# Attention with a routed feed-forward on one core: weights fetched at another round, late projections in halves, first value sets spread

## The chip, the cores and the metric

The kernel runs on one core of one Trainium2 chip. The metric is the device time of one execution in microseconds (us); lower is better. Inputs are float32 and lie in the chip's memory (HBM).

## What is computed

A layer with two branches on one sequence of 2048 tokens of width 128, cut to what matters:

```python
xn = layernorm(x)                                   # 2048 x 128
mod = cos(phase) * amplitude                        # per head and dimension
q, k, v = (xn @ W).split into 16 heads of 8, times mod
scores = q @ k.T / sqrt(8) * cos(2 pi (i - j) / S)  # 16 heads, 2048 x 2048
w = softmax(scores);  w = (w + roll(w, 1, axis=-1)) / sqrt(2)
attention = (w @ v) @ Wo
logits = small softmax mix of xn @ wqkv.T over 8 experts, top 2 per token
ffn = sum over the 2 chosen experts of score * (silu(xn @ w1a.T) * (xn @ w1g.T)) @ w2.T   # F = 352
out = x + attention + ffn
```

The factor cos(2 pi (i - j)/S) is split as cos i cos j + sin i sin j, so each head has 16 rows of q and k (8 dimensions, two rotations). These are stored as float16 high and low parts, 49 rows with a shift row.

## The kernel before, in words

Engines: PE is the matrix engine, PEld its weight load, ACT the activation engine, DVE the vector engine, POOL the general engine, SP the engine that issues most DMAs. All run their own instruction list in order and meet through semaphores.

**Set-up.** `turn_x` makes xnT, `rotate(n)` on PE (L1171 to L1184) makes sixteen projections: i = n // 4 names one of q and k for the first and the second eight heads, c = n % 4 is a quarter of 512 tokens; each is two matrix multiplications of 64 columns of weights by 512 tokens into a PSUM bank from `PROJ_BANKS`. DVE's `rotate(n)` (L782 to L787) multiplies the bank by `mod_up` and cos/sin into `rotated[i]`. Projections 0 to 11 are made in the set-up. Projections 12 to 15 (k of the second eight heads) are made late, one in each of the rounds 10 to 13 (`LATE_AT`), on both engines. They read xnT.

**The rounds.** Attention has 16 heads with 64 score tiles of 128 x 512 each, 1024 tiles in all. Five PSUM banks form a ring; a round r (0 to 204) handles five tiles. In a round PE runs `scores(2r)` (three tiles, banks 0 to 2) and `scores(2r+1)` (two tiles, banks 3 and 4); ACT's `weights(g)` makes one exponential over each group (128x1536, then 128x1024) into `probs`, a ring of 15 tiles in SBUF (L697). `scores(g)` waits until the exponential of group g - 2 is done. Then PE runs `weighted_values(u)` (L1353 to L1376): a piece u is half of a set of four tiles, 4 matrix multiplications of 256 columns with the values as weights (the first set of each head is one piece of 512 columns, u = 0 being empty). Float32 multiplications are two instructions each. `rounds()` (L350 to L376) says which pieces belong to a round: those up to `even = (RING * HALVES * r - NC) // NC`, so 1, 3, 2, 3, 2, 3 pieces in rounds 1 to 6 and from there on 2 and 3 in turn. From round 6 on it is 3 where r is even. ACT's `weights(g)` also waits for the pieces that read the probs it overwrites, from tile 15 (round 3) on: group 6 needs pieces 0 and 1, group 7 pieces 2 and 3, group 9 pieces 4 and 5.

**Work put into the rounds.** After the scores and before the pieces of a round PE does: `rank_tokens` in round 7, the late projections, `square_sums(1)` in round `SECOND_AT` (sums for the ordering of heads and the shifts) and `turn_other(1)` two rounds on. After the pieces it does the expert work. DVE's list has in each round: squares, `copy_out` and `normalise` of the head before (the latter at set k == 2), expert evacuations, then the late rotation and, in the rounds of `PARTS_AT`, `rest(i)`, which makes the two float16 parts of `rotated[i]`. `normalise` writes `attn`, which lies over xnT. DVE runs freely ahead of the rounds; only its semaphores hold it.

**Experts.** Tokens are sorted into 39 tiles of 128 by expert. POOL's `scatter_rows` (L609) writes them to `slots_x` in HBM, one call for each set of four tiles from set 11 to 42, released by that set's pieces. At round 35 (`EXPERTS_AT - 2`, L515) SP waits for all scatters, issues `load_rows(0)` and `load_rows(1)` (L452, eight DMAs), then `stage_weights(0..2)` (w1 and w2 of the first three tiles, L479 and L480, 544 KB a tile, into `staged`, which lies over the stored float16 parts), then `carried` (L522), which DVE's `rows_of_results` reads at round 40. At round 37 it loads the operands of the two exact heads. PE's `widen(0, 0)` (L1281) comes at the end of round 38 and `widen(0, 1)` at the end of 39: they wait for `staged_ld`, `xgT_ready` (DVE's transposition of the loaded rows, L962) and `order_ready`. An expert tile takes four rounds, so the experts run beside the attention from round 38 to the last.

Of the kernel before, what the change touches and what calls it, by code (L numbers as in the profile page):

```python
# [33 lines left out]
ALU = mybir.AluOpType  # L34
# [11 lines left out]
CW = 512  # L46
NC = S // CW
# [12 lines left out]
RING = LARGE_GROUP + SMALL_GROUP  # L60
# [3 lines left out]
QUADS = PER_HEAD // NC  # L64
HALVES = 2
# [13 lines left out]
TOP_EXP_AT = 7  # L79
RANK_AT = 7  # L80
GATES_AT = 8
SECOND_AT = 22
EXPERTS_AT = 37
SCATTER_AT = 11
ROUNDS_A_TILE = 4
LATE_AT = 10
PARTS_AT = (15, 17)
SQUARES_AT = (19, 20)
HALF_HEADS = H // 2
EARLY = HALF_HEADS - EXACT  # L90
EXACT_AT = 156
# [7 lines left out]
PI_DOWN = 3.1415925  # L99
LOWEST = -3.0e38  # L100
EPS = 1e-5
PROJ_BANKS = (2, 3, 0, 1, 2, 3, 0, 1, 2, 3, 0, 1, 7, 5, 7, 5)
SUM_BANKS = (4, 6, 5, 0)
SPREAD = 4.3
ROOT_GUESS = float(0x5F3759DF)
# [11 lines left out]
def build(nc, x, Wq, Wk, Wv, Wo, phase, amp, wqkv, w1, w2, ident_in, desc_in, cs_in, sel_in, tri_in, below_in, count_in, heads_in, earlier_in, of_head_in, places_in, out):  # L117
# [11 lines left out]
    with ExitStack() as ctx:  # L129
# [224 lines left out]
        def rounds():  # L354

            done, j, taken = 0, 0, [0, 0]
            for r in range(ROUNDS + 1):
                w = done // HALVES
                jobs, p = [], w // QUADS
                wanted = jobs_before(p + 1) - j if w % QUADS >= JOB_QUAD else 0  # L360
                half = (RING * r + 1) % 2
                for _ in range(min(wanted, 2 if wanted > (QUADS - w % QUADS) * NC // RING else 1)):
                    if taken[half] == JOBS // 2:
                        half = 1 - half
                    jobs.append((p, j, *job_in(half, taken[half])))
                    taken[half] += 1
                    j += 1
                ready = min(RING * r, SCORE_TILES) // NC * HALVES
                even = (RING * HALVES * r - NC) // NC
                pieces = range(done, max(ready if r == ROUNDS else min(ready, even), done))  # L370
                done = pieces.stop
                yield r, jobs, pieces
# [27 lines left out]
        def _(sp):  # L400
# [81 lines left out]
            def store_shifts(g):  # L482
                sp.wait_ge(shift_ready, g + 1)
                sp.dma_start(shift_rows[HALF_HEADS * g:HALF_HEADS * g + HALF_HEADS, :].rearrange("h (t p) -> (h t) p", p=P),
                             shift[:, g, :]).then_inc(shift_wr, 16)
# [19 lines left out]
            for r, _, _ in rounds():  # L505
                m, step = expert_step(r)
                for p in range(2, PLAIN):
                    issued = groups_for(PER_HEAD * (p - 1))
                    if r == -(-issued // 2):
                        sp.wait_ge(score_ready, issued)  # L510
                        load_head(p)
                if r - 1 in PARTS_AT:
                    for part in range(2):
                        store_part(2 + PARTS_AT.index(r - 1), part)
                if r == SECOND_AT + 3:  # L515
                    store_shifts(1)
                if r == EXPERTS_AT - 2:
                    load_rows(0)
                    load_rows(1)
                    for first in range(STAGES - 1):  # L520
                        stage_weights(first)
                    sp.dma_start(carried[:], slots_x[0:TILES * P, DM:WITH_PLACE].rearrange("(n p) k -> p n k", p=P)).then_inc(carried_ld, 16)  # L522
                if r == EXPERTS_AT:
                    sp.wait_ge(rows_ready, 2)
                    sp.wait_ge(order_ready, 2)
                    for i in range(EXACT):
                        h = sp.value_load(head_order[0:1, PLAIN + i:PLAIN + i + 1], min_val=0, max_val=H - 1)
                        for half in range(2):
                            load_operands(sp, h, qe[:, i, :], ka[:, 2 + i, :], half, exact_ld)
                if step == 1 and m + STAGES - 1 < TILES:  # L530
                    stage_weights(m + STAGES - 1)
                if step == 1 and m % 2 == 1 and m // 2 + 2 < ROW_PAIRS:
                    load_rows(m // 2 + 2)
                if r == EXACT_AT:
                    load_exact_shifts()
# [193 lines left out]
        def _(dve):  # L729
# [52 lines left out]
            def rotate(n):  # L782

                i, c = n // NC, n % NC
                dve.wait_ge(proj_ps, n + 1)
                nc.vector.scalar_tensor_tensor(rotated[i][:, CW * c:CW * c + CW], ps[:, PROJ_BANKS[n], :], mod_up[:, i // 2:i // 2 + 1],  # L786
                                               cs[:, CW * c:CW * c + CW], ALU.mult, ALU.mult).then_inc(rot_ready, 1)  # L787

            def square_late(i):

# [265 lines left out]
            for r, jobs, pieces in rounds():  # L1056
# [14 lines left out]
                for w in quads_in(pieces):  # L1071
                    p, k = w // QUADS, w % QUADS
                    if p >= 1 and k == 0:
                        copy_out(p - 1)
                    if p == 1 and k == 2:
                        dve.wait_ge(x_kept, 16)
                    if p >= 1 and k == 2:
                        normalise(p - 1)
                    if jobs_before(p) < JOBS and jobs_before(p + 1) == JOBS and k == QUADS - 2:
                        make_exact_shift(p)  # L1080
                    if p == H - 1 and k == ADD_AT:
                        add_results()
# [8 lines left out]
                    take_g(m)  # L1091
                if r == RANK_AT:
                    assign_slots()
                if LATE_AT <= r < LATE_AT + 4:
                    dve.wait_ge(rot_ready, 12 + r - LATE_AT)
                    rotate(12 + r - LATE_AT)
                if r in PARTS_AT:
                    dve.wait_ge(rot_ready, 16)
                    rest(2 + PARTS_AT.index(r))
                if r == GATES_AT:  # L1100
                    place_tokens()
# [56 lines left out]
        def _(pe):  # L1158
# [12 lines left out]
            def rotate(n):  # L1171

                i, c = n // NC, n % NC
                g, which = i // 2, i % 2
                if n < 4:
                    pe.wait_ge(xt_ready, max(c + 1, n + 1))
                elif n < 12:
                    pe.wait_ge(rot_ready, n - 3)
                else:
                    pe.wait_ge(rot_ready, max(n - 1, 12))  # L1180
                    pe.wait_ge(slot_ready, 1)
                for half in range(2):
                    ins = nc.tensor.matmul(ps[64 * half:64 * half + 64, PROJ_BANKS[n], :], wmat[:, which, 64 * g:64 * g + 64],  # L1183
                                           xnT[:, CW * c:CW * c + CW], start=True, stop=True, tile_position=(0, 64 * half))  # L1184
                ins.then_inc(proj_ps, 1)

            def values(t):
# [164 lines left out]
            def weighted_values(u):  # L1352
# [4 lines left out]
                cols = slice(HW * half, HW * half + HW)  # L1357
                if half == 0:
                    pe.wait_ge(exp_done, groups_for(tiles[-1] + 1))
                if u == QUADS * HALVES:  # L1360
                    pe.wait_ge(rot_ready, 16)
                if k == 0 and half == 0:
                    pe.wait_ge(vh_ready, p + 1)
                    after(pe, o_copied, p - 1)
# [37 lines left out]
            for r, jobs, pieces in rounds():  # L1402
# [6 lines left out]
                            max_job(*job)  # L1409
                if r == RANK_AT:  # L1410
                    rank_tokens()
                if LATE_AT <= r < LATE_AT + 4:
                    rotate(12 + r - LATE_AT)
                if r == SECOND_AT:
                    pe.wait_ge(slot_ready, 1)
                    square_sums(1)
# [92 lines left out]
```

## Time and profile before

| | us |
|---|---|
| runs before | 593.88, 595.48, 599.56 (median 595.48) |
| the profiled execution | 593.97 |
| its span (first to last instruction) | 592.2 |
| outside the span | 1.77 |
| PE busy | 543.2 (92%) |
| ACT busy | 520.6 (88%) |
| DVE busy | 223.6 (38%) |
| granted clock of PE over the span | 0.983 |

The profile is of one execution. Times in a row are from the start of the span. A row of the timeline merges neighbouring instructions of one line; the bracket is how long the engine sat idle before, and who released it. The granted clock is a share of 2.4 GHz, 0.50 being 1.2 GHz.

### The profile page before, as it was taken

To read this page: it belongs to the slowest core of one execution; us is meant where nothing else is said; L and a number is where in the kernel's file an instruction comes from. 1 tells how busy PE (TensorE), PEld (TensorE's weight loads), DVE (VectorE), ACT (ScalarE), POOL (GpSimd) and SP (SyncE) were. 2 spreads that over 40 slices of the span, in tenths; PEclk is the share of its full clock that TensorE was granted. 3 is DMA by queue.
4 is the path that set the end of the run, shared out by engine and by line. 5 is a ranking of instruction groups with operands and counts; after the bars stand their busy time and mean duration, and the time that the engine had idled before them with its cause. 6 is when DMAs were issued, how large, how long until landed. Compare 5 with 4: busy or idle time off the path is not lost.

```text
span 592.2 us, 19062 instructions
## 1 busy us (share of the span) xinstructions
PE 543.2 (92%) x7948; PEld 255.3 (43%) x7948; DVE 223.6 (38%) x517; ACT 520.6 (88%) x480; POOL 97.3 (16%) x102
## 2 busy tenths in 40 slices
PE   2867998887999999999999999999999999999884
PEld 1342333332444444444445445444544545454333
DVE  7976346500413434344343434334343212221134
ACT  2648989997899999999999999999999999999991
POOL 5210068543001010010101010010101001010000
PEclk9987999999899999999999999999999999999999
DMA  7852035214644232241423233232323313200402
GB/s 220 175 170 94 1 104 145 87 33 126 144 132 128 62 103 78 78 112 48 131 53 96 85 94 96 85 95 66 98 71 95 95 44 94 54 11 7 147 2 74
DMA packets 60890, 53.76 MB, mean 91 GB/s; under 512 B 33244, under 2 KB 50294, under 8 KB 60546
## 3 DMA queue, kind: packets, MB, share of 16 engines
q1 hardware_dynamic: 58082, 47.48, 30.2%
q0 software_dynamic: 2272, 4.72, 2.2%
q8 instruction: 65, 1.06, 0.8%
q10 hardware_dynamic: 448, 0.30, 0.2%
q14 instruction: 23, 0.19, 0.1%
HBM read 38.68 MB, written 13.78 MB: 89 GB/s over the span
## 4 chain that ended last, share of the span: by engine, by line
PE 67%; ACT 13%; issue 11%; DVE 4%; DMA 3%; SPq 1%; POOL 0%; ACTq 0%; DVEq 0%
PE ps L1374 33%; PE ps L1348 21%; ACT big L697 11%; PE ps L1281 7%; PE ps L1291 4%; DMA qk_parts<-store 1%; DVE attnT L761 1%; PE ps L1183 1%; DMA acc<-in_L_attn_x 1%; PE ps L1318 1%; ACT store L654 1%; SPq L452 1%; DMA store<-in_L_ffn_w 1%; DVE big L786 0%; DMA slots_x<-attnT,slot 0%
## 5 line engine op out<-in xcount | busy, mean ns | idle before, releaser
L697 ACT ACTIVATE big<-ps 128x1536 f32<-128x1536 f32 (+1 forms) x410 | 481.4, 1236 | 28.8 <-PE ps L1348 24.7
L1374 PE MATMUL ps<-big,vh 128*32 128x256 f32 (+1 forms) x3968 | 265.7, 394 | 0.0
L1348 PE MATMUL ps<-qa,ka 49*128 49x512 f16 x896 | 166.0, 388 | 19.7 <-ACT big L697 12.9
L1374 PEld LDWEIGHTS ps<-big,vh 128*32 128x32 f32 x3968 | 108.6, 110 | 113.9 <-issue 65.5
L1348 PEld LDWEIGHTS ps<-qa,ka 49*128 49x128 f16 x896 | 37.5, 94 | 139.2 <-ACT big L697 107.5
L593 POOL DMA_INDIRECT results<-y,row_of x39 | 37.9, 971 | 270.8 <-DVE y L984 269.4
L1281 PE MATMUL ps<-xgT,store 128*32 128x128 f32 x1716 | 66.5, 276 | 2.8 <-DMA store<-in_L_ffn_w 2.8
L1281 PEld LDWEIGHTS ps<-xgT,store 128*32 128x32 f32 x1716 | 55.0, 112 | 18.4 <-issue 6.0
L969 DVE SCALAR_TENSOR_TENSOR cs<-cs,ps 128x384 f32<-128x384 f32 x39 | 21.6, 554 | 91.9 <-ACT cs L689 91.9
L1047 DVE TENSOR_REDUCE m<-ps 128x1 f32<-128x512 f32 x64 | 44.1, 689 | 31.2 <-PE ps L1385 31.2
L984 DVE TENSOR_SCALAR y<-ps,weight_of 128x128 f32<-128x128 f32 x39 | 13.7, 351 | 98.2 <-PE ps L1291 98.2
L609 POOL DMA_INDIRECT slots_x<-attnT,slot x32 | 36.0, 1126 | 52.6 <-PE ps L1374 50.2
L978 DVE SCALAR_TENSOR_TENSOR cs<-cs,ps 128x384 f32<-128x384 f32 x39 | 21.6, 554 | 40.5 <-PE ps L1281 40.5
L1291 PE MATMUL ps<-store,cs 128*32 128x128 f32 (+1 forms) x936 | 32.8, 273 | 0.0
L1291 PEld LDWEIGHTS ps<-store,cs 128*32 128x32 f32 (+1 forms) x936 | 27.2, 110 | 6.7
L587 POOL COPY vh<-vaug 128x144 f32 x16 | 8.1, 508 | 120.0 <-PE ps L1374 99.0
L1348 PE MATMUL ps<-attnT,ka 49*128 49x512 f16 x128 | 24.0, 383 | 3.9 <-ACT big L697 3.6
L689 ACT ACTIVATE cs<-ps 128x384 f32<-128x384 f32 x39 | 19.1, 490 | 5.7 <-PE ps L1281 5.7
L1385 PE MATMUL ps<-ka,attnT 49*128 49x512 f16 x64 | 24.1, 376 | 0.0
L962 DVE STREAM_TRANSPOSE xgT<-cs 128x128 f32<-128x128 f32 x39 | 11.8, 302 | 23.5 <-DMA cs<-slots_x 23.5
L1029 DVE COPY osb<-ps 128x512 f32<-128x512 f32 x16 | 11.0, 687 | 21.1 <-PE ps L1374 21.1
L1183 PE MATMUL ps<-xnT,wmat 128*64 128x512 f32 x64 | 16.7, 633 | 0.0
(186 smaller groups left out, 201.9 us busy)
## 6 DMA issues: line engine op xcount, KB each, us to landing
store<-in_L_ffn_w SPq DMA_DIRECT2D x39, 352.0 KB, 3.1
store<-in_L_ffn_w SPq DMA_DIRECT2D x39, 192.0 KB, 3.4
qk_parts<-store SPq DMA_DIRECT2D x8, 512.0 KB, 4.1
qa<-qk_parts SPq DMA_DIRECT2D x27, 128.0 KB
slots_x<-vh SPq DMA_DIRECT2D x8, 330.0 KB, 7.6
cs<-slots_x SPq DMA_DIRECT2D x80, 32.0 KB, 2.7
store<-results SPq DMA_DIRECT2D x4, 512.0 KB, 5.6
ka<-qk_parts SPq DMA_DIRECT2D x31, 64.0 KB, 2.4
```

What stands on the lines that cost most here:

```text
L593: nc.gpsimd.indirect_dma_start(results, bass.IndirectOffsetOnAxis(ap=row_of[:, m:m + 1], axis=0), y[:, m % 4, :], None).then_inc(y_wr[m % ...
L609: nc.gpsimd.indirect_dma_start(slots_x, bass.IndirectOffsetOnAxis(ap=slot[:, r, t:t + 1], axis=0), xn_placed[:, t, :], None).then_inc(scat ...
L697: nc.scalar.activation(probs[:, prob_of(tiles[0]):prob_of(tiles[-1]) + 1, :], ps[:, bank_of(tiles[0]):bank_of(tiles[-1]) + 1, :], ACT.Exp, ...
L969: nc.vector.scalar_tensor_tensor(turned_gate[:, k, :], turned_gate[:, k, :], 1.0, ps[:, SIDE_BANK, 0:FP], ALU.add, ALU.mult).then_inc(a_ta ...
L978: nc.vector.scalar_tensor_tensor(hidT[:, k, :, :].rearrange("p f s -> p (f s)"), turned_gate[:, k, :], 0.5, ps[:, SIDE_BANK, 0:FP], ALU.mu ...
L1047: nc.vector.tensor_reduce(m4[:, NT * r + i, c:c + 1], ps[:, O_BANKS[(p - 1) % 2], :], AX, ALU.max).then_inc(m_reduced, 1)
L1183: ins = nc.tensor.matmul(ps[64 * half:64 * half + 64, PROJ_BANKS[n], :], wmat[:, which, 64 * g:64 * g + 64], xnT[:, CW * c:CW * c + CW], s ...
L1281: ins = nc.tensor.matmul(ps[c:c + 32, SIDE_BANK, P * f:P * f + P], w1_of[m % STAGES][:, F * b + f0 + c:F * b + f0 + c + 32], xgT[:, m % 2, ...
L1291: ins = nc.tensor.matmul(ps[c:c + 32, SIDE_BANK, FP:FP + DM], hidT[0:n, m % 2, f, c:c + 32], w2_of[m % STAGES][0:n, f, :], start=f == 0, s ...
L1348: ins = nc.tensor.matmul(ps[:, bank_of(n), :], k[at:at + KQ, P * o:P * o + P], q[at:at + KQ, CW * c:CW * c + CW], start=True, stop=True, t ...
L1374: ins = nc.tensor.matmul(ps[32 * c:32 * c + 32, O_BANKS[p % 2], cols], vh[:, p % 2, o + 8 * b, :], probs[:, prob_of(n), cols], start=k == ...
L1385: nc.tensor.matmul(ps[:, O_BANKS[(p - 1) % 2], :], qe[at:at + KQ, r, P * i:P * i + P], near_keys(ka[at:at + KQ, 2 + r, :], i), start=True, ...
```

## The change

First, `stage_weights(0..2)` is issued at round 28 (`STAGE_AT`) instead of round 35, ahead of the row loads. Second, each of projections 12 to 15 is made as two halves of 256 tokens, eight halves over rounds 10 to 17, all in one bank (`SIDE_BANK`, halves alternating), and `rest(3)`, the squares, the square sums and what follows come one round later; the wait before the values of the second head goes. `normalise(0)` moves from set 2 to set 7 of the second head (round 16 to round 20), since it overwrites what the late halves still read. Third, `even` is lowered by 2, 1 and 1 in rounds 2, 3 and 4: the pieces are 1, 1, 3, 3, 3, 3 in rounds 1 to 6 in place of 1, 3, 2, 3, 2, 3.

```diff
-SECOND_AT = 22
+SECOND_AT = 23
 LATE_AT = 10
-PARTS_AT = (15, 17)
-SQUARES_AT = (19, 20)
+LATE = 2 * (16 - 12)
+ROTATIONS = 12 + LATE
+PARTS_AT = (15, 18)
+SQUARES_AT = (20, 21)
+STAGE_AT = 28
+FIRST_NORMALISED = 7
-PROJ_BANKS = (2, 3, 0, 1, 2, 3, 0, 1, 2, 3, 0, 1, 7, 5, 7, 5)
+PROJ_BANKS = (2, 3, 0, 1, 2, 3, 0, 1, 2, 3, 0, 1)
-                even = (RING * HALVES * r - NC) // NC
+                even = (RING * HALVES * r - NC) // NC - (2, 1, 1)[r - 2] if 2 <= r < 5 else (RING * HALVES * r - NC) // NC
...
+                if r == STAGE_AT:
+                    for first in range(STAGES - 1):
+                        stage_weights(first)
                 if r == EXPERTS_AT - 2:
                     load_rows(0)
                     load_rows(1)
-                    for first in range(STAGES - 1):
-                        stage_weights(first)
...
+            def rotate_late(j):
+
+                n, side = 12 + j // 2, j % 2
+                i, first = n // NC, CW * (n % NC) + HW * side
+                dve.wait_ge(proj_ps, 12 + j + 1)
+                nc.vector.scalar_tensor_tensor(rotated[i][:, first:first + HW], ps[:, SIDE_BANK, HW * side:HW * side + HW], mod_up[:, i // 2:i // 2 + 1],
+                                               cs[:, first:first + HW], ALU.mult, ALU.mult).then_inc(rot_ready, 1)
...
-                    if p == 1 and k == 2:
+                    if p == 1 and k == FIRST_NORMALISED:
                         dve.wait_ge(x_kept, 16)
-                    if p >= 1 and k == 2:
+                    if p >= 1 and k == (FIRST_NORMALISED if p == 1 else 2):
                         normalise(p - 1)
...
-                if LATE_AT <= r < LATE_AT + 4:
+                if LATE_AT <= r < LATE_AT + LATE:
                     dve.wait_ge(rot_ready, 12 + r - LATE_AT)
-                    rotate(12 + r - LATE_AT)
+                    rotate_late(r - LATE_AT)
                 if r in PARTS_AT:
-                    dve.wait_ge(rot_ready, 16)
+                    dve.wait_ge(rot_ready, (12, ROTATIONS)[PARTS_AT.index(r)])
                     rest(2 + PARTS_AT.index(r))
...
+            def rotate_late(j):
+
+                n, side = 12 + j // 2, j % 2
+                i, first = n // NC, CW * (n % NC) + HW * side
+                pe.wait_ge(rot_ready, 12 + j)
+                pe.wait_ge(slot_ready, 1)
+                for half in range(2):
+                    ins = nc.tensor.matmul(ps[64 * half:64 * half + 64, SIDE_BANK, HW * side:HW * side + HW],
+                                           wmat[:, i % 2, 64 * (i // 2):64 * (i // 2) + 64], xnT[:, first:first + HW],
+                                           start=True, stop=True, tile_position=(0, 64 * half))
                 ins.then_inc(proj_ps, 1)
...
-                if u == QUADS * HALVES:
-                    pe.wait_ge(rot_ready, 16)
...
-                if LATE_AT <= r < LATE_AT + 4:
-                    rotate(12 + r - LATE_AT)
+                if LATE_AT <= r < LATE_AT + LATE:
+                    rotate_late(r - LATE_AT)
```

## Rows read from the trace of the kernel before

**Rows 1.** The page: busy time of each engine, and the chain that ended last.

```profile
PE 543.2 (92%) x7948; PEld 255.3 (43%) x7948; DVE 223.6 (38%) x517; ACT 520.6 (88%) x480; POOL 97.3 (16%) x102
...
PE 67%; ACT 13%; issue 11%; DVE 4%; DMA 3%; SPq 1%; POOL 0%; ACTq 0%; DVEq 0%
```

**Rows 2.** Timeline of ACT, rounds 2 to 6: start, length, merged count, idle before.

```profile
49.53 2.37 ACT L697 ACTIVATE big<-ps 128x1536 f32<-128x1536 f32 x2 [0.28 <-PE ps L1348]
53.97 4.62 ACT L697 ACTIVATE big<-ps 128x1536 f32<-128x1536 f32 x4 [2.07 <-PE ps L1348]
58.78 4.62 ACT L697 ACTIVATE big<-ps 128x1536 f32<-128x1536 f32 x4 [0.19 <-PE ps L1348]
```

**Rows 3.** Timeline of PE, rounds 2, 3 and 6.

```profile
48.49 1.44 PE L1348 MATMUL ps<-qa,ka 49*128 49x512 f16 x5 [1.76 <-ACT big L697]
49.85 3.54 PE L1374 MATMUL ps<-big,vh 128*32 128x512 f32 x24
53.33 0.82 PE L1348 MATMUL ps<-qa,ka 49*128 49x512 f16 x5
...
61.20 0.39 PE L1348 MATMUL ps<-qa,ka 49*128 49x512 f16 x2 [0.31 <-ACT big L697]
```

**Rows 4.** Busy time by stretch: length, engines, granted clock, DMA share, GB/s.

```profile
49.80:53.40 3.60, 3.60 (x28) 1.06 (x28) 3.37 (x7) 2.10 (x2) 0.00 (x0) 0.53 0.00 0
...
116.00:130.00 14.00, 12.31 (x150) 4.47 (x150) 0.47 (x3) 13.44 (x13) 7.12 (x8) 1.00 0.11 36
...
145.90:151.80 5.90, 5.90 (x65) 3.10 (x65) 0.56 (x1) 2.85 (x3) 0.32 (x1) 0.50 1.06 175
```

**Rows 5.** Timeline of ACT, rounds 8 to 16.

```profile
65.97 7.07 ACT L697 ACTIVATE big<-ps 128x1536 f32<-128x1536 f32 x6
74.23 2.37 ACT L697 ACTIVATE big<-ps 128x1536 f32<-128x1536 f32 x2 [1.20 <-PE ps L1348]
76.99 2.37 ACT L697 ACTIVATE big<-ps 128x1536 f32<-128x1536 f32 x2 [0.40 <-PE ps L1348]
...
82.94 6.89 ACT L697 ACTIVATE big<-ps 128x1536 f32<-128x1536 f32 x6 [0.40 <-PE ps L1348]
```

**Rows 6.** Timeline of PE and DVE: a late projection, its rotation, and rest(2).

```profile
71.15 1.08 PE L1183 MATMUL ps<-xnT,wmat 128*64 128x512 f32 x4
...
72.36 0.75 DVE L786 SCALAR_TENSOR_TENSOR second<-ps,mod_up,cs 128x512 f32<-128x512 f32 x1 [2.62 <-PE ps L1183]
...
84.37 1.22 DVE L778 CAST store<-second 128x2048 f16<-128x2048 f32 x1
...
85.62 2.29 DVE L780 TENSOR_TENSOR store<-second,store 128x2048 f16<-128x2048 f32 x1
```

**Rows 7.** Timeline of ACT, the exponentials of rounds 23 and 25.

```profile
104.95 4.62 ACT L697 ACTIVATE big<-ps 128x1536 f32<-128x1536 f32 x4 [0.68 <-PE ps L1348]
110.02 4.62 ACT L697 ACTIVATE big<-ps 128x1536 f32<-128x1536 f32 x4 [0.45 <-PE ps L1348]
```

**Rows 8.** Timeline of SP, DVE and PE where the experts begin.

```profile
136.59 3.94 SPq L452 DMA_DIRECT2D cs<-slots_x  x8
...
140.13 0.31 DVE L962 STREAM_TRANSPOSE xgT<-cs 128x128 f32<-128x128 f32 x1 [23.51 <-DMA cs<-slots_x]
...
145.90 1.50 PE L1281 MATMUL ps<-xgT,store 128*32 128x128 f32 x22 [2.76 <-DMA store<-in_L_ffn_w]
...
153.82 0.23 DVE L1005 TENSOR_TENSOR choice<-carried,places_h 128x39 f32<-128x39 f32 x1 [0.67 <-DMA carried<-slots_x]
...
159.10 0.83 PE L1281 MATMUL ps<-xgT,store 128*32 128x128 f32 x22
```

**Rows 9.** Timeline of ACT, the exponentials of rounds 39 and 40.

```profile
148.40 2.36 ACT L697 ACTIVATE big<-ps 128x1536 f32<-128x1536 f32 x2 [0.46 <-PE ps L1348]
...
152.63 4.63 ACT L697 ACTIVATE big<-ps 128x1536 f32<-128x1536 f32 x4 [1.86 <-PE ps L1348]
```

More of the change, by code:

```diff
@@ L1176, in rotate @@
                     pe.wait_ge(xt_ready, max(c + 1, n + 1))
-                elif n < 12:
+                else:
                     pe.wait_ge(rot_ready, n - 3)
-                else:
-                    pe.wait_ge(rot_ready, max(n - 1, 12))
-                    pe.wait_ge(slot_ready, 1)
                 for half in range(2):
@@ L1184, in rotate @@
                                            xnT[:, CW * c:CW * c + CW], start=True, stop=True, tile_position=(0, 64 * half))
+                ins.then_inc(proj_ps, 1)
+            def rotate_late(j):
[7 more added lines that the diff above has]
+                                           start=True, stop=True, tile_position=(0, 64 * half))
                 ins.then_inc(proj_ps, 1)
```

## The prediction

> **What bounds the kernel now.** First the page: PE is busy 92% and ACT 88% of the span [rows 1], so both are near the limit, and the chain of work that ended last runs through PE for 67% and ACT for 13%. Then the waits and the timeline of ACT and PE, stage by stage, since the shares are averages. In the plain rounds the two engines hold each other. ACT needs 2.25 us a round when it never waits (four exponentials end after 4.62, two after 2.37), but after each second round it waits 0.19 for PE, so two rounds take 4.81 us, or 2.405 each [rows 2]. The reason is in PE's rows: the two-tile scores can start only when ACT has ended the last group of the round before, PE idles 0.31 for that [rows 3], and with three pieces behind them PE delivers the next scores 0.31 later than ACT would like. So a plain round of three pieces takes 2.56 and one of two pieces 2.25, with about 0.3 of room in the latter. Whatever is put on PE in a three-piece round is paid in full, and in a two-piece round all but 0.3.
>
> Four places cost more than the plain rounds, and the change is at all four. (a) Round 2: ACT idles 2.07 before the exponential of round 3 [rows 2]. (b) Rounds 10 to 13: idle 1.20 before round 11, 0.40 before rounds 12 and 14 [rows 5]. (c) Rounds 22 and 24: idle 0.68 and 0.45 [rows 7]. (d) Rounds 38 and 39: PE stands 2.76 for the first expert weights [rows 8]; ACT's exponentials of rounds 39 and 40 begin at 148.40 and 152.63, where a plain pace would be near 143.7 and 146.1 [rows 9].
>
> **Part by part, against the profiled execution's 593.97 (span 592.2 and 1.77 around it).**
>
> *(d) Expert weights at round 28.* SP issues the row loads at 136.59, then the six weight DMAs. DVE has the first rows at 140.13; PE reaches `widen(0,0)` at 145.90 - 2.76 = 143.14, so rows are there 2.7 us early, and only the weights are late [rows 8]. In the gap the granted clock goes down: 1.00 before, and 0.50 (1.2 GHz) from 145.90 to 151.80 [rows 4]. So the wait is paid twice. The 22 expert multiplications take 1.50 in the slow stretch and 0.83 in a fast one [rows 8]. With the weights there, `widen` runs from 143.14 for 0.76, and the three-tile scores come 0.64 later (half of the 1.04 from 48.49 to 49.53 is 0.52 [rows 3, 2], plus a semaphore's 0.1): the exponential of round 39 starts at 144.55 in place of 148.40, a gain of 3.85. The round from there to the next took 152.63 - 148.40 = 4.23 [rows 9]; at full clock it is scores 0.82 [rows 3], two pieces about 1.0 (two thirds of three pieces, 1.43) and `widen` 0.76, 2.58 in all: a gain of 1.65. Sum 5.5. What comes next: the idle is gone, so the clock should stay at 1.00. What is late next is `carried`: issued after the weights, it landed near 153.8 [rows 8], 7.9 after its issue. Now it is issued near 141, and PE will need the result of it (`result_out(0)`) some 7 us into the new schedule of round 39 on, near 153: even 7.9 us of latency and DVE's 3 us fit, with about 1 to 2 to spare. Bounds: 0 if another wait of the same length comes in its place, 5.8 if the round falls to 2.3. I take 5.5, since each term is a duration from a row. The six DMAs themselves move to near 117 us, where DMA is busy 0.11 [rows 4]; SP has nothing queued between the load of the fourth head (round 26) and round 35, so no one waits behind them. Their condition (float16 parts stored, squares made) is met by round 22.
>
> The Trainium skill (Trainium Kernel Development and Optimization, Key Constraints) says that DMAs of all queues run on the same 16 engines and interleave; by it the 1.6 MB burst would slow POOL's scatters of rounds 28 to 32, a rival below. No row here shows the two together.
>
> *(a) First value sets.* Round 2 now holds one piece of 512 columns (8 instructions) for three pieces (24), which took 3.54 at a clock of 0.53 [rows 3, 4]. In columns the first piece is half of it, 1.7. PE is then free at 49.85 + 1.7 = 51.55; the three-tile scores take 1.04 at half clock: round 3 starts at 52.6 instead of 53.97, 1.4 earlier. Then it gives some back: round 3 has three pieces, and its second exponential waits for pieces 2 and 3, which end at about 54.2 where ACT would be ready at 53.95 (0.3 lost). Rounds 3, 4, 5 and 6 all hold three pieces, where rounds 3 and 5 held two. Followed round by round with 2.18 of bare PE time for three pieces (3.19 of the late rounds less 1.01), plus 0.15 to 0.25 of waiting for ACT, rounds 4, 5, 6 and 7 start at 55.25, 57.65, 60.0 and 62.4. Before, round 7 started at 58.78 + 4.62 + 0.19 = 63.6 [rows 2]. Gain 1.2. Bounds: 0.3 and 1.4.
>
> *(b) Late projections.* One took 1.08 on PE [rows 6], 1.01 net of overlap; a half takes 0.51. Before, from the start of round 10 (65.97 + 7.07 - 2.37 = 70.67) to round 14 at 82.94 are 12.27 us [rows 5], against 9.62 for four plain rounds: 2.65 too many, of which 0.3 came back, since rounds 14 to 16 ran 6.89 without a wait. Net 2.35. After: a three-piece round (10, 12, 14, 16) takes 2.56 + 0.51 = 3.07. The two-piece round behind it is bare PE time, 1.75 + 0.51 = 2.26. Eight rounds take 4 x 5.33 = 21.3, against 19.24 plain: 2.05 too many. So eight halves cost nearly what four wholes did: the room in two-piece rounds is used, but the 0.31 wait for ACT, which vanished when PE was far behind, comes back four times. Gain 0.3. Bounds: -0.5 and +0.9. DVE's side: the half rotation is below the whole's 0.75 [rows 6]; I take 0.42 (0.75 halved and a fixed part). The lower end is a new wait: `rest(2)` (1.22 + 2.29 [rows 6]) stands in DVE's list between the rotations of rounds 15 and 16. From the start of PE's round 15, DVE ends half 5 at 1.9, `rest(2)` at 5.45 and half 6 at 5.9, and PE asks for it in round 17 at 2.26 + 3.07 + 0.82 = 6.15. It fits by 0.2. Behind that instruction on PE stand the pieces of round 17 and all that follows. The removed wait for 16 rotations cost nothing (ACT and PE show no idle at round 14). `normalise(0)` in round 20 costs nothing: its reader is `copy_out(1)`, seven rounds on.
>
> *(c) Square sums and transposition* move from rounds 22 and 24 (three pieces) to 23 and 25 (two pieces). Cost now 0.68 + 0.45 less twice 0.19, 0.75 [rows 7]. In two-piece rounds 0.3 of each is free: 0.2 and 0 are left. Gain 0.45; bounds 0 and 0.75. DVE's work between the two leaves the transposition about 0.3 of room.
>
> Sum: 5.5 + 1.2 + 0.3 + 0.45 = 7.45, so 593.97 - 7.45 = 586.5 for an execution like the profiled one, and 595.48 - 7.45 = 588.0 against the median, which is 1.5 higher. I predict the middle, 587.3. After round 40 PE is the engine without a gap, so nothing later should give time back.
>
> **The rivals.**
>
> *R1, another wait takes the weights' place.* The last scatter (slowed by the burst), the row loads or `carried` come too late, PE stands again and the clock falls again. For it: the burst is 1.6 MB, and the row chain has only 2.7 us of room. Against: the last scatter is seven rounds after the burst, DMA is at 0.11 there, and POOL has idle time to catch up. Then (d) gives 0 to 1.5 and the others 1.95: 590.5 to 592.0, or up to 593.5 by the median.
>
> *R2, only the weights count.* The phases of PE and ACT eat (a), (b) and (c), and the halves cost 0.5 more by DVE's late half 6. For it: the eight halves fall on four rounds that have no room. 593.97 - 5.5 + 0.5 = 589.0, to 590.5 by the median.
>
> *R3, slower.* The clock rose only in the unbroken 3.54 us of PE work of round 2 [rows 3, 4]; rounds 0 and 1, with breaks over 1 us, left it at half. The change cuts just this block to 1.7. If the rise then comes late, each round of three pieces takes 4.36 in place of 2.41, 1.95 more. The point from which it decides is 7.45 / 1.95, nearly four rounds; at six rounds the time is 593.97 - 6.25 + 11.7 = 599.4. Against: the scores of round 3 and its pieces follow without a break, so PE is busy from 48.49 to 54.6 all the same. The Trainium skill (TensorE: Matmul & The Clock Gate, Part 1) says the moment of the rise differs from run to run; this trace shows one run and cannot bear that out.
>
> That the change does not do what it says (SP held at round 28) is excluded: the squares it waits for stand seven rounds ahead in DVE's list, the stores nine ahead in its own.
>
> **How the numbers follow.** Forecast 0.66 (585.0 to 589.5, its own range, from the bounds of the four terms), R1 0.16, R2 0.13, R3 0.05. The range 585.0 to 592.5 takes in R2 and most of R1. About 1% (5.95 us, so 589.5) is what a measurement of this kernel can tell from no change. Faster by more: the forecast, 0.66. Within 1%: R1, R2 and the short half of R3, 0.31. Slower: 0.03.
>
> **What would show it.** Round 3's exponential at 52.6 and round 7's at 62.4. From round 10 to round 18, 21.3 us, with ACT idle 0.7 after each even round and near 0 after the odd ones. Idle after rounds 23 and 25 of 0.2 or less. No wait of PE for `in_L_ffn_w` or `slots_x`, the clock 1.00 throughout, the expert multiplications 0.83 from the first on, the two exponentials after round 38 2.6 apart. Wrong would be: a wait of PE for `xgT` or DVE's `y`, a granted clock of 0.50 after 54 us, or later rounds that take longer than before.

## The result and the profile after

The changed kernel takes 588.57 us (four times, 586.17 to 589.13) against 594.93 for the kernel before (four, 593.88 to 599.56): ratio 0.9876, 95% interval 0.9839 to 0.9912. So it is 1.2% faster, 7.4 us by the ratio. The forecast was 587.3, and a sum of 7.45. The sum agrees with the 7.4, but the interval alone reaches from 5.2 to 9.6 us, and not all of its terms hold.

The page of the profile after (span 587.1), the same two lines as [rows 1]:

```profile
PE 544.6 (93%) x7964; PEld 258.0 (44%) x7964; DVE 222.0 (38%) x521; ACT 521.4 (89%) x480; POOL 93.9 (16%) x102
...
PE 69%; issue 12%; ACT 12%; DVE 3%; DMA 2%; SPq 1%; ACTq 0%; DVEq 0%
```

PE's busy time is the same within 1.4 us (543.2 before): no work went away, only waiting. The timeline of ACT after, answering to [rows 2, 5, 7, 9]:

```profile
47.44 2.37 ACT L702 ACTIVATE big<-ps 128x1536 f32<-128x1536 f32 x2 [0.28 <-PE ps L1370]
50.70 1.45 ACT L702 ACTIVATE big<-ps 128x1536 f32<-128x1536 f32 x1 [0.89 <-PE ps L1370]
52.58 3.28 ACT L702 ACTIVATE big<-ps 128x1024 f32<-128x1024 f32 x3 [0.43 <-PE ps L1394]
...
60.86 2.37 ACT L702 ACTIVATE big<-ps 128x1536 f32<-128x1536 f32 x2 [0.19 <-PE ps L1370]
...
71.07 4.74 ACT L702 ACTIVATE big<-ps 128x1536 f32<-128x1536 f32 x4 [0.77 <-PE ps L1370]
76.47 4.70 ACT L702 ACTIVATE big<-ps 128x1536 f32<-128x1536 f32 x4 [0.66 <-PE ps L1370]
...
87.25 9.44 ACT L702 ACTIVATE big<-ps 128x1536 f32<-128x1536 f32 x8 [0.70 <-PE ps L1370]
97.65 4.62 ACT L702 ACTIVATE big<-ps 128x1536 f32<-128x1536 f32 x4 [0.96 <-PE ps L1370]
...
137.03 4.62 ACT L702 ACTIVATE big<-ps 128x1536 f32<-128x1536 f32 x4 [0.19 <-PE ps L1370]
...
142.49 7.17 ACT L702 ACTIVATE big<-ps 128x1536 f32<-128x1536 f32 x6
149.94 2.37 ACT L702 ACTIVATE big<-ps 128x1536 f32<-128x1536 f32 x2 [0.27 <-PE ps L1370]
```

The same view of the kernel before, where [rows 5, 9] do not show it, had these two waits besides:

```profile
80.18 2.37 ACT L697 ACTIVATE big<-ps 128x1536 f32<-128x1536 f32 x2 [0.82 <-PE ps L1348]
...
147.45 0.49 ACT L689 ACTIVATE cs<-ps 128x384 f32<-128x384 f32 x1 [3.92 <-PE ps L1281]
```

The idle of 2.07 before round 3 is now 0.89, with 0.43 inside the round. The four idles before rounds 11 to 14 (1.20, 0.40, 0.82, 0.40) are now one of 0.66 to 0.77 every second round. The 3.92 and 1.86 at the experts are gone. Stages run from the start of one round's first exponential to that of another. In the two profiled executions they are (us; rounds 7 to 10, left out, take 7.06 in both):

| stage | before | after | gain | forecast |
|---|---|---|---|---|
| up to round 0 | 43.70 | 41.60 | 2.10 | 0 |
| rounds 0 to 7 | 19.90 | 19.26 | 0.64 | 1.2 |
| rounds 10 to 18 | 21.61 | 21.66 | -0.05 | 0.3 |
| rounds 18 to 27 | 22.57 | 23.12 | -0.55 | 0.45 |
| rounds 27 to 37 | 24.07 | 24.32 | -0.25 | 0 |
| rounds 37 to 42 (first experts) | 18.77 | 12.91 | 5.86 | 5.5 |
| round 42 to the first copy of the tail | 423.70 | 423.66 | 0.04 | 0 |
| from there to the end | 10.83 | 13.50 | -2.67 | 0 |

At the experts, all is as forecast. PE goes from the last value piece straight into `widen`, at full clock (PE after, answering to [rows 8]; the second row is `widen(0, 1)`):

```profile
141.09 0.84 PE L1303 MATMUL ps<-xgT,store 128*32 128x128 f32 x22
...
143.49 0.84 PE L1303 MATMUL ps<-xgT,store 128*32 128x128 f32 x22
```

The loss that nobody forecast is in the last row of the table. PE's tail after, and the stretch's granted clock (the column before the DMA share and GB/s):

```profile
567.71 2.80 PE L1394 MATMUL ps<-big,vh 128*32 128x256 f32 x48
572.90 2.65 PE L1334 MATMUL ps<-ident,xnT 128*128 128x128 f32 x16 [2.39 <-DVE xnT L1056]
...
576.23 6.03 PE L1340 MATMUL ps<-wo_mod,attnT 128*128 128x128 f32 x32 [0.56 <-ACT attnT L710]
```

```profile
570.00:587.00 17.00, 9.31 (x62) 8.20 (x54) 6.12 (x14) 2.25 (x4) 0.00 (x0) 0.72 0.23 65
```

PE stands 2.39 us for DVE's normalisation of the last head, the clock falls, and the output projection takes 6.03 us. The same gap stood in the kernel before, but in its profiled execution the clock held and the projection took 3.84:

```profile
580.67 1.97 PE L1312 MATMUL ps<-ident,xnT 128*128 128x128 f32 x16 [2.39 <-DVE xnT L1043]
...
583.47 3.84 PE L1318 MATMUL ps<-wo_mod,attnT 128*128 128x128 f32 x32 [0.71 <-ACT attnT L705]
```

So the two profiles differ in three things that the forecast did not have: the set-up (2.10 gained), ACT's late start at round 21 (0.96 idle for 0.19, 0.8 lost) and the tail (2.67 lost). Together they lose 1.3 us, which is part of why the two profiled executions lie only 5.05 us apart.

### The profile page after: what moved, and what is told of

It is laid out like the page before. It is cut to its first block, busy times and chain, and to the rows that moved or that the text cites. A ratio compares the mean times of both kernels' runs of the same rounds, so it can differ in the third digit from the quotient of the medians.

```text
span 587.1 us, 19106 instructions
## 1 busy us (share of the span) xinstructions
PE 544.6 (93%) x7964; PEld 258.0 (44%) x7964; DVE 222.0 (38%) x521; ACT 521.4 (89%) x480; POOL 93.9 (16%) x102
## 3 DMA queue, kind: packets, MB, share of 16 engines
q8 instruction: 65, 1.06, 0.8%
## 4 chain that ended last, share of the span: by engine, by line
PE 69%; issue 12%; ACT 12%; DVE 3%; DMA 2%; SPq 1%; ACTq 0%; DVEq 0%
PE ps L1394 32%; PE ps L1370 21%; ACT big L702 12%; PE ps L1303 7%; PE ps L1313 4%; PE ps L1193 1%; PE ps L1340 1%; DMA acc<-in_L_attn_x 1%; DMA qk_parts<-store 1%; DVE store L785 1%; PE ps L1181 1%; PE ps L1204 0%; PE ps L1334 0%; DMA qa<-shift_rows 0%; PE ps L1226 0%
## 5 line engine op out<-in xcount | busy, mean ns | idle before, releaser
L1303 PE MATMUL ps<-xgT,store 128*32 128x128 f32 x1716 | 65.2, 273 | 0.0
L592 POOL COPY vh<-vaug 128x144 f32 x16 | 5.5, 341 | 111.4 <-PE ps L1394 93.9
L975 DVE STREAM_TRANSPOSE xgT<-cs 128x128 f32<-128x128 f32 x39 | 11.8, 303 | 23.6 <-DMA cs<-slots_x 23.6
L1370 PEld LDWEIGHTS ps<-attnT,ka 49*128 49x128 f16 x128 | 5.5, 93 | 22.0 <-ACT big L702 19.1
```

The costliest lines, as they stand in the source:

```text
L1303: ins = nc.tensor.matmul(ps[c:c + 32, SIDE_BANK, P * f:P * f + P], w1_of[m % STAGES][:, F * b + f0 + c:F * b + f0 + c + 32], xgT[:, m % 2, ...
L1370: ins = nc.tensor.matmul(ps[:, bank_of(n), :], k[at:at + KQ, P * o:P * o + P], q[at:at + KQ, CW * c:CW * c + CW], start=True, stop=True, t ...
```

## The experiments

They ran on three chips, four kernels a time: e1 to e4 on the first, e5 to e8 on the second, e9 to e12 on the third. Which chip the first two profiles come from is not known. Each ratio is to the kernel before on the same chip (medians 595.64, 592.45 and 594.5), so only ratios are compared between the three. Stage times are from the profiles, and "tail" is from the first copy of the tail to the end.

**e1, the weights alone.** In the kernel before:

```diff
+                if r == 28:
+                    for first in range(STAGES - 1):
+                        stage_weights(first)
                 if r == EXPERTS_AT - 2:
...
-                    for first in range(STAGES - 1):
-                        stage_weights(first)
```

> The kernel before with one edit: the first three weight sets are issued at round 28. Theory (the weights are most of the gain): PE does not wait for them, the granted clock stays at 1.00 through rounds 38 and 39, and from the exponential of round 37 to that of round 42 it takes 12.9 us as in the changed kernel, against 18.8 before; the whole is 5.5 to 6 us faster, ratio near 0.990. Rival (the four parts share the gain, or the weights collide with the scatters): less than 3 us, and a wait of PE for rows in place of the one for weights.

Measured: ratio 0.9918 (0.9890 to 0.9946), 4.9 us. Rounds 37 to 42 take 12.92:

```profile
142.02 4.62 ACT L699 ACTIVATE big<-ps 128x1536 f32<-128x1536 f32 x4 [0.19 <-PE ps L1350]
146.97 0.49 ACT L691 ACTIVATE cs<-ps 128x384 f32<-128x384 f32 x1 [0.33 <-PE ps L1283]
147.49 7.17 ACT L699 ACTIVATE big<-ps 128x1536 f32<-128x1536 f32 x6
154.94 2.37 ACT L699 ACTIVATE big<-ps 128x1536 f32<-128x1536 f32 x2 [0.27 <-PE ps L1350]
```

No wait took the place of the one removed. The theory holds. The size of 4.9 is below the expected 5.5 to 6, but the interval (3.2 to 6.6 us) takes that in. What the missing weights cost also varies: the four profiles without the early weights take 17.63 (e3), 17.93 (e5), 18.77 (the first) and 19.33 (e2) for these rounds, the ten with them all 12.91 or 12.92. So the gain is 4.7 to 6.4 by the execution.

**e2, the rest without the weights**: the changed kernel, with `stage_weights` back behind the row loads at round 35 (e1's edit undone).

> The changed kernel with the first weights back at round 35: only the spread value sets, the half projections and their followers are left. Theory, from the two traces: the early sets give 0.65 us (rounds 2 to 7), the halves nothing (rounds 10 to 18 take 21.6 both ways) and the followers nothing or a small loss: 0 to 1 us faster than before, ratio 0.998 to 1.000. Rival, the sum of the prediction: 1.95 us faster, ratio 0.9967.

Measured: 0.9951 (0.9927 to 0.9976), 2.9 us (1.4 to 4.3), three times what the theory allowed. The number fits the rival (0.9967), its mechanism does not: rounds 0 to 7 give 0.8 (19.07 against e3's 19.84), not 1.2, and the halves give nothing of their own (e6). What stands out between the two profiles is rounds 17 to 37: 49.45, against 51.14 in e3. But two profiles do not settle the 2.9, since at the experts e2's took 1.7 more than e3's. With e1 it makes 0.9918 x 0.9951 = 0.9869, and the changed kernel has 0.9876: the parts add, within their intervals.

**e3, the kernel before again**, unchanged.

> The kernel before, unchanged, for a second profile of it. Theory (the 2.65 us that the changed kernel's profiled execution lost after the last exponential, and the 2.1 us that it gained before the first, are differences between executions): here too the set-up or the tail may differ from the first profile by 1 to 3 us, while round 2 to 7 take 14.07, rounds 10 to 18 21.6 and round 37 to 42 18.8 us again. Rival (set-up and tail are fixed by the program): both equal the first profile within 0.3 us.

Measured: ratio 0.9989 (0.9966 to 1.0013). The set-up took 40.67 (43.70 in the first profile), the tail 11.92 (10.83), and the stages inside the rounds differ too: 17 to 37 take 51.14 (48.88), and 37 to 42 take 17.63 (18.77). Theory and rival were both partly wrong: the first profile is one draw of a kernel whose clock falls in several places, now here and now there. This is e3 in round 22 and at the experts, as stretches:

```profile
100.00:101.00 1.00, 1.00 (x24) 0.66 (x27) 0.00 (x0) 0.00 (x0) 0.27 (x1) 1.00 0.18 63
101.00:102.00 1.00, 1.00 (x16) 0.67 (x12) 0.48 (x2) 0.72 (x1) 0.18 (x1) 0.61 0.02 4
102.00:103.00 1.00, 1.00 (x12) 0.29 (x4) 0.90 (x4) 1.00 (x2) 0.79 (x1) 0.50 0.06 16
103.00:104.00 1.00, 1.00 (x9) 0.23 (x5) 0.90 (x4) 0.65 (x1) 0.51 (x1) 0.50 0.22 68
...
140.00:150.00 10.00, 6.68 (x88) 3.17 (x91) 0.56 (x1) 5.37 (x6) 0.00 (x0) 0.83 0.83 182
150.00:151.00 1.00, 1.00 (x23) 0.40 (x11) 0.49 (x2) 0.55 (x1) 0.32 (x1) 1.00 1.00 28
```

The clock is at 1.2 GHz from 101.2 to 104.6, which the first profile does not show, and back at 2.4 GHz by 150 at the experts, where in the first profile it stayed down until 151.80 [rows 4], so that the same missing weights cost 1.1 us less. Ahead of the fall in round 22, PE had idled 0.85 and 0.31, because ACT began late (0.79 idle):

```profile
97.52 2.37 ACT L697 ACTIVATE big<-ps 128x1536 f32<-128x1536 f32 x2 [0.79 <-PE ps L1348]
101.28 2.37 ACT L697 ACTIVATE big<-ps 128x1536 f32<-128x1536 f32 x2 [1.40 <-PE ps L1348]
```

e1 shows the same fall (104.0 to 107.4) and takes 51.67 for rounds 17 to 37. On the same chip e2 and e4 do not, and take 49.45 and 49.69, nor does the profile after (49.78). That is 1.7 us between e2's profile and e3's. That it happens beyond the profiles is likely and not shown by stage: the granted clock over the whole span is above 0.980 in 6 of 26 executions of the kernel before on this chip, and in 9 of 12 of e2. Nor does a gap alone bring the fall: e9 idled 1.69 and 0.31 at the same place, more than e3, and its clock stayed up.

**e4, a busy tail.** In the changed kernel, before the last projections:

```diff
+            def keep_busy(n):
+                for _ in range(n):
+                    nc.tensor.matmul(ps[:, SIDE_BANK, 0:P], ones[:], ident[:], start=True, stop=True)
...
             def project_all(r):
+                if r == 0:
+                    pe.wait_ge(y_copied, TILES)
+                    keep_busy(9)
```

> The changed kernel with nine extra float32 multiplications of 128 columns on PE after the last value piece, into a bank that nobody reads, while it would wait 2.4 us for the last head's normalisation. Theory (the clock falls in the tail because of that gap): the granted clock stays at 1.00 to the end, from the first copy of the transposed attention to the end 10.8 us as in the kernel before, against 13.5; 0 to 2.6 us faster than the changed kernel, whose four times lay between 586.17 and 589.13. Rival (the fall has another cause, or the extra work is itself in the way): the clock falls all the same, or the tail is 0.2 to 1 us longer.

Measured: 0.9842 (0.9812 to 0.9871), 586.10, five of six times between 585.89 and 586.24. The changed kernel did not run on this chip; e10 has the comparison. Tail 10.8.

```profile
570.50 2.27 PE L1345 MATMUL ps<-ident,ones 128*128 128x128 f32 x18
...
572.96 1.97 PE L1334 MATMUL ps<-ident,xnT 128*128 128x128 f32 x16 [0.18 <-DVE xnT L1056]
...
575.76 3.84 PE L1340 MATMUL ps<-wo_mod,attnT 128*128 128x128 f32 x32 [0.71 <-ACT attnT L710]
```

```profile
573.00:577.00 4.00, 3.29 (x29) 3.02 (x30) 1.29 (x6) 2.05 (x4) 0.00 (x0) 1.00 0.00 0
```

The projection is back at 3.84. The extra work fills the gap and delays nothing: `xnT` is still what PE waits for (0.18).

**e5, the square sums one round later, alone.**

```diff
-SECOND_AT = 22
+SECOND_AT = 23
```

> The kernel before with one edit: SECOND_AT 23 for 22, so that the square sums, the transposition and what follows fall in rounds with two value pieces. Theory (in most executions the kernel before loses 1.6 to 1.9 us between rounds 21 and 27 to a fall of the granted clock beside the square sums of round 22, and the move avoids it): the clock stays at 1.00 there, rounds 21 to 27 take about 15 us instead of 16.8 to 17.1, and the whole is 1.5 to 2.3 us faster, ratio 0.9965. Rival (the move gives only the free 0.3 us twice, and the clock falls or not by chance): 0.2 to 0.5 us.

Measured: 0.9986 (0.9969 to 1.0004), 0.8 us, which the times alone do not tell from nothing. On this chip ACT is not late at round 21 and no clock falls there; rounds 17 to 37 take 48.13 (48.13 or 48.14 in e6 and e8 too), against 48.88 in the first profile of the kernel before, and the idles of 0.68 and 0.45 behind the two operations are at most 0.19. So by stage the move is worth 0.75 where nothing else happens: all that the two operations had cost, not the 0.45 of the forecast. The theory of 1.5 to 2.3 could not be tested here, since the kernel before does not seem to have the fall on this chip either (granted clock 0.983 or 0.984 in 12 of 17 executions, as in the first profile); whether this edit or another of the change prevents the fall in round 22 where ACT is late stays open.

**e6, whole projections.** e1's kernel, with `SECOND_AT = 23`, the lowered `even` of rounds 2 to 4 and e4's tail.

> The changed kernel with the busy tail, but the late projections whole again, in rounds 10 to 13, with parts and squares where they were before; weights at 28, the spread value sets and SECOND_AT 23 stay. Theory (the halves give nothing: 21.6 us for rounds 10 to 18 both ways): the same time as with halves and busy tail, 586.1, within 0.5 us. Rival (the halves are worth the 1.5 to 2 us that the change without the weights gained beyond its early sets, by keeping PE without gaps): 587.5 or more, with a fall of the clock between rounds 17 and 27.

Measured: 0.9846 (0.9824 to 0.9869), against 0.9842 for the halves with the same tail on another chip. Within one chip, the profiles of e6 and e8 (halves) take 21.61 and 21.66 for rounds 10 to 18. Halving is worth nothing by itself. Whether it would be on a chip whose ACT starts late was not tried.

**e7, halves in odd rounds.** In e4's kernel:

```diff
-SECOND_AT = 23
+SECOND_AT = 29
-PARTS_AT = (15, 18)
-SQUARES_AT = (20, 21)
-STAGE_AT = 28
-FIRST_NORMALISED = 7
+PARTS_AT = (15, 26)
+SQUARES_AT = (20, 27)
+STAGE_AT = 33
+FIRST_NORMALISED = 15
+LATE_ROUNDS = tuple(range(11, 27, 2))
```

with `r in LATE_ROUNDS` for the late rounds on PE and DVE.

> The changed kernel with the busy tail and the eight halves only in rounds of two value pieces (11, 13 to 25), the parts at 15 and 26, squares at 20 and 27, square sums at 29, weights at 33. Theory (a two-piece round has 0.3 us of room or more: the 0.5 us of square sums there cost nothing in the changed kernel): each half costs 0 to 0.3 us in place of 0.29 on the mean, rounds 10 to 29 are 1 to 2 us shorter, 584.1 to 585.1. Rival (the room is 0.3 and the rest is paid, or DVE's later squares and weights stand in the way): within 0.5 us of 586.1 or slower.

Measured: 0.9831 (0.9808 to 0.9853), 582.77, with e6 at 583.48 and e8 at 583.56 on this chip: 0.7 to 0.8 us faster, between theory (1 to 2) and rival (0.5), and less than the intervals can tell. Each pair of rounds with a half takes 4.97:

```profile
84.70 4.62 ACT L703 ACTIVATE big<-ps 128x1536 f32<-128x1536 f32 x4 [0.34 <-PE ps L1378]
89.67 4.63 ACT L703 ACTIVATE big<-ps 128x1536 f32<-128x1536 f32 x4 [0.34 <-PE ps L1378]
```

A half costs 0.16 there (a plain pair takes 4.81), and 0.30 in consecutive rounds (21.66 less 19.24, over eight). Rounds 10 to 29 take 46.8 against 48.2 in e6 and e8, as the theory said. PE then waited 0.64 for DVE's `sel` at round 29, and rounds 10 to 37 take 66.5 against 67.5. The profiled execution (585.49) is the slowest of six: its round 0 starts at 44.02, against 41.48 in e6.

**e8, a warm start.** In e4's kernel, `fill(n, bank)` issues n of the same multiplications: 6 into bank 4 behind an added wait for `square_ready` and, after the wait for `v_ready`, 3 into bank 7, all ahead of the first round, then

```diff
+                if r < 2:
+                    fill((3, 5)[r], O_BANKS[1])
                 if r == RANK_AT:
```

> The changed kernel with the busy tail and extra float32 multiplications of 128 columns on PE into banks nobody reads: nine before round 0, where PE waits for the first operands, three after the scores of round 0 and five after those of round 1. Theory (the clock is at half through rounds 0 to 3 because of these gaps): the granted clock reaches 1.00 before round 2, ACT's idle before round 3 (0.89 us) and within it (0.43) falls below 0.3 in sum, 1 to 1.6 us faster than 586.1. Rival (the rise does not depend on these gaps, or the extra work delays the scores): no gain or up to 1 us slower, the clock still 0.50 in round 2.

Measured: 0.9849 (0.9826 to 0.9871), 583.56, so no gain over e6 in the medians. The profiled execution took 581.21, the four others 583.54 to 583.78. In the profiled one (granted clock 0.999 over the span, 0.996 in the others) the clock is at 1.00 before round 0 and stays there, and rounds 0 to 7 take 17.68 in place of 19.36 in e6:

```profile
40.00:45.00 5.00, 3.55 (x26) 2.27 (x24) 3.09 (x4) 4.95 (x5) 0.00 (x0) 1.00 0.50 180
```

**e9 to e12** ran together on the third chip. e9 is the changed kernel, e10 is e4's kernel, both again; e11 is e7's kernel with `SECOND_AT = 31`; e12 is e11's with e8's edit.

> The changed kernel, unchanged, for its times and a second profile beside those of the versions with a busy tail. Theory (the clock often falls in its tail): 2 to 2.7 us slower than with the busy tail where it falls, and its times spread by 2 to 3 us; ratio to the kernel before 0.987 to 0.990. Rival (the tail is kept by chance only): the same time as with the busy tail within 0.5 us.

> The changed kernel with nine extra multiplications in the tail, as before, now on the chip on which the changed kernel itself is timed. Theory: 1.5 to 2.7 us faster than it, ratio to the kernel before 0.984 to 0.985, spread of the times under 1 us but for single ones. Rival: no difference.

> Halves in the rounds 11, 13 to 25 and busy tail, with the square sums at round 31 instead of 29 (in the version with 29, PE waited 0.64 us there for DVE's scaled sums). Theory: no wait there, ACT's idle after round 29 at most 0.2, rounds 10 to 31 0.4 us shorter, and 1.4 to 1.9 us faster than the changed kernel with busy tail. Rival (halves in odd rounds pay elsewhere): less than 0.7 us faster.

> The version with halves in odd rounds, square sums at 31 and busy tail, with the warm start added (nine extra multiplications ahead of round 0, three in round 0, five in round 1). Theory (the clock at half in rounds 0 to 3 costs ACT time): round 0 to round 7 take 17.7 us in place of 19.3, and the whole is 1.3 to 1.7 us faster than without the warm start, in every execution. Rival (the executions that were not profiled, equal to the version without it on the same chip, are the rule; the gain is given back in the tail or elsewhere): within 0.5 us of it.

| | median (range) | ratio, 95% interval | up to round 0 | rounds 0 to 7 | 10 to 37 | tail |
|---|---|---|---|---|---|---|
| e9 | 588.37 (587.4 to 589.36) | 0.9895 (0.9871 to 0.9920) | 40.96 | 18.90 | 69.88 | 11.8 |
| e10 | 585.33 (584.98 to 586.87) | 0.9852 (0.9825 to 0.9880) | 40.63 | 18.89 | 69.09 | 10.9 |
| e11 | 586.29 (585.02 to 586.84) | 0.9853 (0.9826 to 0.9880) | 44.29 | 18.63 | 67.65 | 10.8 |
| e12 | 584.53 (584.0 to 584.91) | 0.9827 (0.9800 to 0.9853) | 43.13 | 17.68 | 67.72 | 10.8 |

e10 against e9 confirms the busy tail: 3.0 us, and no time of one reaches the other. The profiled tails differ by 0.9 and the first transpositions ahead of them by 0.45; the rest of the 3.0 is not shown by this pair, whose profiles also differ by 0.8 in rounds 10 to 37 (ACT's late start at round 21).

e11 missed: its times overlap those of e10, its ratio is the same, its median 1.0 slower. Its rounds 10 to 37 are 1.4 us shorter, but its set-up ended 3.7 us later in the profiled execution. The set-up ends near 41 or near 44 in the same code (40.67 and 43.70 for the kernel before); whether the other executions of e11 share the late one is open. And the move of the square sums did not pay: rounds 10 to 31 take 51.62 against 52.07 in e7, as expected, but rounds 10 to 37 take 67.65 against 66.5, since ACT idles 0.79 before round 32 and 1.06 before round 34, where PE waits 0.98 for DVE's `other` (0.82, 1.09 and 1.01 in e12).

e12 is 1.8 us faster than e11 and faster in every execution, so the warm start does pay here. Of the 2.1 between the two profiles, 0.95 lies in rounds 0 to 7 and 1.16 ahead of round 0. Yet in e12 the clock was already at half when the extra work began, and nine multiplications took 4.19 us (2.25 in e8), over the time at which the operands came: the scores of round 0 start 5.1 us after the load of the first shift rows was issued (37.00), in e11, where PE waits for that load, 2.8 (40.46 to 43.24).

```profile
37.94 4.19 PE L1429 MATMUL ps<-ident,ones 128*128 128x128 f32 x18
42.06 1.46 PE L1378 MATMUL ps<-qa,ka 49*128 49x512 f16 x5
```

None of its times reaches one of e10 or e11. e12 has the lowest ratio of all, 0.9827, beside 0.9876 and 0.9895 for the changed kernel; e7's 0.9831, from another chip, is not clear of it.

## Why the prediction was right or wrong

**(d) The weights: right, mechanism and size.** Forecast 5.5, found 5.86 between the profiles. The point that decided was that the clock's fall is part of the wait's price. The two terms were 3.85 and 1.65; measured, round 39 starts 4.04 us nearer to round 37 (5.46 for 9.50), and from round 39 to 42 it takes 7.45 for 9.27, 1.82 less. e1 gives 4.9 in the ratio, and by the profiles the wait removed cost 4.7 to 6.4. `carried` was no wait (DVE read it at 145.46 without idle). POOL's scatters of rounds 27 to 36 took 0.97 us each in the profile after, as in the first. So R1 is refuted. What the burst may have cost is small: with the weights at round 28, rounds 27 to 37 take 24.26 to 24.36 on the first and third chip and in the profile after (ACT idle 0.38 to 0.48 before round 31), and 24.07 without it; on the second chip it is 24.07 with it too (e6, e8).

R2, that only the weights count, did not come either: the rest alone gives 2.9 us (e2).

**(a) The early sets: right in kind, twice too large.** Forecast 1.2, found 0.64, and 0.8 between e3 and e2; no run has this part alone. The step that failed is the following of rounds 2 to 4. Eight instructions took 1.93 at half clock where 1.7 was put, the stall inside round 3 was 0.43 for 0.3, and round 4 took 2.56 for 2.4: three sizes too small, one after the other. R3 did not come: the clock was back at 51.8, before the end of round 3's pieces (52.9).

**(b) The halves: the forecast of nearly nothing was right.** 0.3 forecast, -0.05 found. The list of waits left out the 0.82 before round 13, but the 12.27 of the sum holds it. A half took 0.65 on PE, 0.58 net, in place of 0.51 (so two rounds took 5.4, not 5.33), and DVE 0.48 for 0.42. The wait feared for DVE's half 6 did not come. The argument that the wait for ACT comes back four times holds: ACT idles 0.66 to 0.77 before rounds 11, 13, 15 and 17, and with the halves in odd rounds (e7) at most 0.34, once in two rounds.

**(c) The square sums: too small, and its follower unforeseen.** The step "In two-piece rounds 0.3 of each is free" undersized the room: the 0.49 of the square sums cost nothing there, and by stage the move is worth 0.75 (e5). In the profile after, it is hidden by ACT's late start at round 21 (0.96 idle) and 0.53 that PE waited at round 25 for DVE's `other`. The room named for that was there on the second chip (no wait in e5, e6 and e8). In the profile after, DVE began to read the sums 1.2 us after the last of their multiplications had started; in the first profile it was 0.2 (the kernel before first, then the changed one):

```profile
102.39 0.56 PE L1204 MATMUL ps<-sel,second 128*128 128x8 bf16 x16
102.98 0.29 DVE L821 COPY mean_square<-ps 128x128 f32<-128x128 f32 x1 [5.03 <-PE ps L1204]
```

```profile
102.65 0.56 PE L1226 MATMUL ps<-sel,second 128*128 128x8 bf16 x16
104.27 0.29 DVE L834 COPY mean_square<-ps 128x128 f32<-128x128 f32 x1 [4.38 <-PE ps L1226]
```

**What no step had** was that the first profile is one draw. "After round 40 PE is the engine without a gap" passed over the gap of 2.39 in the tail, behind which the clock falls in some executions: the tail takes 10.8 and 11.9 us in the two profiles of the kernel before, 13.5 and 11.8 in those of the changed one. And on the first chip of the experiments the profiles of the kernel before lose about 2 us more from round 17 to 37, with a fall of the clock at round 22 (e1, e3), and those of the changed kernel's versions do not. Whether such a difference is part of the 7.4 us is open; the pair of the result does not show it.

With each term at its real size the sum is 7.2 (5.86 + 0.64 - 0.05 + 0.75), near the forecast because (d) and (c) were put 0.4 and 0.3 too low and (a) and (b) 0.6 and 0.35 too high. That errors cancel so well, and that the measured 7.4 falls on it although the interval is 2 us wide to either side, is luck.

## What to carry to other kernels

A long wait on PE (2.39 and 2.76 us here) may have to be paid twice, once as idle time and once as half clock behind it; look at the granted clock after each such gap, in more than one profile. Where it can't be removed, a few multiplications into an unused bank can fill it at no cost (3.0 us faster here), provided that they end before the real work is due. Work moved between stages of two coupled engines should go where the other engine ends last, here the rounds of two pieces; cutting it into equal parts over all rounds gave nothing.

## What the runs showed of the hardware that was not expected

Where ACT waits for the scores of a round, its exponential starts 0.41 us after the third score multiplication did, at full clock. At round 21 it started 1.0 to 1.9 us after it in e1 to e4, e9, e10 and the profile after (ACT idle 0.79 to 1.63). On the second chip (e5, e6, e8) and in the first profile of the kernel before it was 0.41 (idle 0.19). In e11 and e12, with halves in rounds 19 and 21, ACT does not idle before round 21. The multiplications themselves show no such delay.

It is not ACT alone. DVE read the square sums 0.8 to 1.2 us after the last of their multiplications had started in e1 to e4, e9, e10 and the profile after, and 2.3 and 2.4 us in e11 and e12, where this made PE wait at round 33. On the second chip and in the first profile it was 0.2. The cause is not seen. The rounds before round 21 hold the stores of the float16 parts, but so they do on the second chip.

The clock's fall after a gap is not the same in each execution. After the gap of 2.39 us in the tail it stayed up in the first profile of the kernel before and in e2, and fell in e3, e1, e5, e9 and the profile after, with tails of 10.8 to 13.5 us from the same instructions. The Trainium skill (TensorE: Matmul & The Clock Gate, Part 1) says of the clock's rise that it comes after a different number of multiplications from run to run of the same kernel. These runs agree: in the changed kernel the clock rose 10.2 us after the start of round 0 in the profile after (at 51.8) and 9.4 us after it in e9 (at 50.3).
